# Attention and feed-forward layer in one kernel: softmax shifts transposed in groups of two pairs of heads, shorter leads, beginning reordered

## The reference

```python
x = query                                        # (32, 256, 128) float32
h = (x - mean(x)) / sqrt(var(x) + 1e-5)
q = einsum('bnd,hde->bhne', h, Wq) / 8           # 16 heads of 64
k = einsum('bmd,hde->bhme', h, Wk)
v = einsum('bmd,hde->bhme', h, Wv)
attn = softmax(einsum('bhne,bhme->bhnm', q, k), axis=-1)
o = einsum('bhnm,bhme->bnhe', attn, v)
x = x + dot(swapaxes(o, -1, -2).reshape(B, N, 1024), Wp) + bp
y = layernorm(layernorm_plain(x)) * ln1_g + ln1_b
y = gelu_tanh(y @ ternary(w1).T + b1)            # hidden width 512
y = layernorm(y) * ln2_g + ln2_b
x = x + y @ ternary(w2).T + b2                   # ternary(w): -1, 0 or 1 times mean |w|
```

## Time and profile before

| | us |
|---|---|
| median of 3 runs | 1002.18 (1001.26 to 1003.38) |
| span of the profiled execution, first to last instruction | 998.7 |
| PE busy | 980.8 (98%) |
| DVE busy | 880.0 (88%) |
| POOL busy | 837.1 (84%) |
| ACT busy | 729.6 (73%) |

### The profile page before, as it was taken

How to read it: one execution, slowest core, us unless ns; L and a number is a source line. 1 busy time by engine, 2 the same in 40 slices (tenths; PEclk the granted TensorE clock), 3 DMA queues, 4 the chain that set the end, 5 groups by cost and what they waited for, 6 DMA issues and landing times.

```text
span 998.7 us, 39391 instructions
## 1 busy us (share of the span) xinstructions
PE 980.8 (98%) x16052; PEld 782.2 (78%) x16052; DVE 880.0 (88%) x1779; ACT 729.6 (73%) x1151; POOL 837.1 (84%) x861
## 2 busy tenths in 40 slices
PE   7899999999999999999999999999999999999998
PEld 6577777778777787887887777888878777788886
DVE  7888988988889888898889988889889988788998
ACT  5687677777767777777777777777777776879995
POOL 6789888989887888888899888888888889866765
PEclk9999999999999999999999999999999999999999
DMA  6112332222331232233222233324222233354343
GB/s 141 38 32 51 53 66 45 43 49 52 74 53 27 51 73 53 52 53 71 55 48 41 48 73 51 53 53 71 46 41 47 52 52 53 69 86 75 77 86 65
DMA packets 203682, 57.82 MB, mean 58 GB/s; under 512 B 185072, under 2 KB 203248, under 8 KB 203504
## 3 DMA queue, kind: packets, MB, share of 16 engines
q1 hardware_dynamic: 201424, 54.79, 29.8%
q10 hardware_dynamic: 2080, 0.52, 0.2%
HBM read 7.21 MB, written 4.19 MB: 11 GB/s over the span
## 4 chain that ended last, share of the span: by engine, by line
PE 95%; DVE 2%; ACT 1%; issue 1%; POOL 1%; DVEq 0%; POOLq 0%; ACTq 0%
PE S L675 11%; PE PV L700 8%; PE M L635 7%; PE PV L702 6%; PE PV L701 6%; PE QK L622 5%; PE QK L623 5%; PE QK L624 5%; PE misc L675 5%; PE S L667 5%; PE S L864 3%; PE M L753 2%; PE M L718 2%; PE M L754 2%; PE M L755 2%; PE misc L667 2%
## 5 line engine op out<-in xcount | busy, mean ns | idle before, releaser
L1210 POOL TENSOR_TENSOR pl<-p 128x1024 f16<-128x1024 f32 x253 | 476.9, 1896 | 39.3 <-ACT p L1000 39.1
L1410 DVE TENSOR_REDUCE negmax<-M 128x4 f32<-128x1024 f32 x252 | 306.8, 1217 | 22.4 <-PE M L635 16.4
L1008 ACT ACTIVATE QKh<-QK 128x512 f16<-128x512 f32 x251 | 149.5, 596 | 155.5 <-PE QK L624 155.3
L1000 ACT ACTIVATE p<-S,s_exp 128x1024 f32<-128x1024 f32 x173 | 192.4, 1112 | 71.8 <-PE S L675 71.2
L700 PEld LDWEIGHTS PV<-V,p 128*128 128x128 bf16 x2048 | 186.8, 98 | 46.4 <-issue 34.5
L700 PE MATMUL PV<-V,p 128*128 128x65 f16 x2048 | 214.9, 194 | 4.0 <-DVE O L1424 2.9
L701 PE MATMUL PV<-V,p 128*128 128x64 f16 x2048 | 213.4, 193 | 0.0
L702 PE MATMUL PV<-V,pl 128*128 128x65 f16 x2048 | 212.6, 194 | 0.0
L1430 DVE TENSOR_TENSOR QKl<-QK,QKh 128x512 f16<-128x512 f32 x251 | 172.4, 687 | 42.2 <-ACT QKh L1008 41.1
L701 PEld LDWEIGHTS PV<-V,p 128*128 128x128 bf16 x2048 | 189.1, 97 | 4.7
L702 PEld LDWEIGHTS PV<-V,pl 128*128 128x128 f16 x2048 | 188.7, 97 | 0.0
(11 more groups left out here) (236 smaller groups left out, 2501.6 us busy)
## 6 DMA issues: line engine op xcount, KB each, us to landing
result<-X SPq DMA_DIRECT2D x15, 256.0 KB, 2.6
X<-in_L_attn_query SPq DMA_DIRECT2D x7, 512.0 KB, 4.8
OT<-O SPq DMA_TRANSPOSE x64, 4.6
shift<-negmax SPq DMA_TRANSPOSE x63, 2.3
O<-in_L_attn_Wk ACTq DMA_DIRECT2D x2, 256.0 KB, 4.3
O<-in_L_attn_Wq SPq DMA_DIRECT2D x2, 256.0 KB, 4.5
O<-in_L_attn_Wv SPq DMA_DIRECT2D x1, 512.0 KB, 3.9
w<-in_L_ffn_w SPq DMA_DIRECT2D x2, 256.0 KB, 5.6
```

The source lines that it names most:

```text
L1000: e.activation(p32[r][:, :, :, :].rearrange("p i m n -> p (i m n)"), score_bank(p)[:, :], ACT.Exp, scale=s_exp[:, :]).then_inc(s_ex, 1)
L1210: e.tensor_tensor(pl[r][:, :, :, :].rearrange("p i m n -> p (i m n)"), p32[r][:, :, :, :].rearrange("p i m n -> p (i m n)"), p_high(r).rea ...
L1410: e.tensor_reduce(dst[:, :, NB * jj:NB * jj + NB], max_bank(p)[:, :].rearrange("p (i t m) -> p i t m", i=2, t=NB), AX.X, ALU.max, negate=T ...
```

## The change

Groups have two pairs in place of four (`GP`). Queries and keys are computed five pairs ahead in place of seven, maxima four in place of six. Before step 0 three further pairs are started (`FIRST`) in place of five. The constants that hang on these move with them: `PAIRED`, `LOW_ON_DVE`, the banks of the first pairs. In the beginning ACT scales and splits the weight pieces 2 and 3 earlier and rounds pairs in another order; the statistics and the split of batch 2's input move from steps 0 to 5 to steps 4 to 7; the reduction of the projection weights (`part_p`, `part_g`) moves from the beginning into step 9, and turning and spreading follow in steps 10 and 11 in place of 7 and 8. `shift_in` becomes a semaphore for each buffer.

```diff
-GP = 4
+GP = 2
-Q_LEAD, MAX_LEAD, PV_LAG = 7, 6, 3
+Q_LEAD, MAX_LEAD, PV_LAG = 5, 4, 3
-PAIRED = NP - 6
+PAIRED = NP - 4
-LOW_ON_DVE = (NP - 5, NP - 3, NP - 1)
+LOW_ON_DVE = (NP - 3, NP - 1)
-MAXIMA = {"pg": (None, 7, 8), "t1": (45, 46, 54)}
+MAXIMA = {"pg": (9, 10, 11), "t1": (45, 46, 54)}
-FIRST = 5
+FIRST = 3
@@ def qk_pairs(t):
-    first = {0: [5, 6], 1: [7, 8], 2: [9], TWO_1: []}
+    first = {0: [4, 5], TWO_1: []}
@@ def max_pairs(t):
-    first = {0: ([], [5]), 1: ([6], [7])}
+    first = {0: ([], [3]), 1: ([4], [5])}
@@ def x_stats_batch(b, j):
-    return b + 2 if j == (2 if in_two(HP * b) else 0) and 1 <= b + 2 < B else None
+    return b + 2 if j == (2 if in_two(HP * b) else 0 if b else 4) and 1 <= b + 2 < B else None
...
@@ def qk_bank(p):
-            return PV if p in (1, 4, 6, 8) else QK
+            return PV if p in (1, 4) else QK
@@ def scores(p):
-                    e.wait_ge(shift_in, 16 * g)
+                    e.wait_ge(shift_in[g % 2], shift_turned(g))
@@ pe_program, beginning
+            max_scores(2)
             queries_keys(3)
-            max_scores(2)
-            e.wait_ge(s_mx, 2)
-            kept_busy(3)
-            max_scores(3)
-            queries_keys(4)
             first_shift_turned()
-            max_scores(4)
@@ act_program, beginning
             qk_high(0)
+            w_high(2)
             qk_high(1)
             qk_high(2)
-            w_high(2)
+            w_high(3)
+            first_shift()
             qk_high(3)
             x_high(1)
-            qk_high(4)
-            w_high(3)
-            first_shift()
@@ pool_program, beginning
             w_low(2)
+            w_low(3)
             x_low(1)
-            w_low(3)
-            add_bp(0)
...
+            add_bp(0)
             add_bp(1)
@@ dve_program, beginning
             max_out(2)
-            max_out(3)
-            max_out(4)
-            for p in range(2, FIRST):
-                qk_low(p)
-            e.wait_ge(p_in, P_IN)
-            largest_of(3, t2_rows(Wp), "part_p")
-            e.wait_ge(ffn_in, FFN_IN)
-            largest_of(4, g2[:, :], "part_g")
+            qk_low(2)
+            qk_low(3)
```

More of the change, by code:

```diff
@@ L104, in x_stats_batch @@
 def x_stats_batch(b, j):
-    return b + 2 if j == (2 if in_two(HP * b) else 0) and 1 <= b + 2 < B else None
+    return b + 2 if j == (2 if in_two(HP * b) else 0 if b else 4) and 1 <= b + 2 < B else None
 def x_norm_tile(b, j):
-    return (b + 2, j - 1) if j in (1, 2) and 2 <= b + 2 < B else None
+    first = 1 if b else 5
+    return (b + 2, j - first) if j in (first, first + 1) and 2 <= b + 2 < B else None
 def x_split_batch(b, j):
-    return b + 2 if j == (5 if in_two(HP * b) else 3) and 1 <= b + 2 < B else None
+    return b + 2 if j == (5 if in_two(HP * b) else 3 if b else 7) and 1 <= b + 2 < B else None
 def x_bias_batch(b, j):
-    return b + 2 if j == (7 if in_two(HP * b) else 5) and 1 <= b + 2 < B else None
+    return b + 2 if j == (7 if in_two(HP * b) or b == 0 else 5) and 1 <= b + 2 < B else None
 def two_values(t):
@@ L244, in qk_bank_before @@
 def qk_bank_before(p):
-    first = {0: None, 1: None, 2: None, 3: 0, 4: 1, 5: 3, 6: 4, 7: 5, 8: 6, 9: 7, 10: 9}
+    first = {0: None, 1: None, 2: None, 3: 0, 4: 1, 5: 3, 6: 5}
     return first.get(p, p - 1)
@@ L347, in layer @@
         ot_in = [sem(f"s_outputs_transposed{c}") for c in range(H // HH)]
-        xt_in, shift_in = sem("s_x_transposed"), sem("s_shift_transposed")
+        xt_in = sem("s_x_transposed")
+        shift_in = [sem(f"s_shift_transposed{i}") for i in range(2)]
         yt_in = [sem(f"s_ffn_y_transposed{i}") for i in range(2)]
@@ L409, in qk_bank @@
                 return misc_banks[misc_bank_no("qk", 2)]
-            return PV if p in (1, 4, 6, 8) else QK
+            return PV if p in (1, 4) else QK
         def max_bank(p):
-            return S if p in (1, 3) else M
+            return S if p == 1 else M
         def score_bank(p):
@@ L429, in two_free, with shift_turned @@
             return (s_x0, first_tiles(b)) if tile == 0 else (s_x1, b + 1)
+        def shift_turned(g):
+            return 16 * ((g + 1) // 2)
         def head_rows(i):
@@ L531, in turn_shift @@
                 e.dma_start_transpose(shift[g % 2][:, :].unsqueeze(1),
-                                      negmax16[g % 2][:, :, :].rearrange("p i c -> p (i c)")).then_inc(shift_in, 16)
+                                      negmax16[g % 2][:, :, :].rearrange("p i c -> p (i c)")).then_inc(shift_in[g % 2], 16)
             def turn_y(g):
@@ L692, in weighted @@
                 else:
-                    e.wait_ge(s_qklo, 9)
+                    e.wait_ge(s_qklo, 5)
                 for t in range(NB):
@@ L986, in shift_rounded @@
                 if g >= 3:
-                    e.wait_ge(shift_in, 16 * (g - 2))
+                    e.wait_ge(shift_in[g % 2], shift_turned(g - 2))
                 elif g == 1:
@@ L1472, in weights @@
             def weights(t):
+                if t == MAXIMA["pg"][0]:
+                    e.wait_ge(p_in, P_IN)
+                    largest_of(3, t2_rows(Wp), "part_p")
+                    e.wait_ge(ffn_in, FFN_IN)
+                    largest_of(4, g2[:, :], "part_g")
                 if t == SUMS:
```

## The result

Over 20 executions each the changed kernel took 1003.27 us (1001.69 to 1005.81) against 1001.42 (1000.80 to 1003.38): a ratio of 1.0018 with an interval of 1.0012 to 1.0024. The forecast was 1000.1, faster. The change is slower by 1.9 us, where it should have won 2.1.

The account below looks back on a forecast made before the run. PE was taken as the bound, busy 99.79 of 100 us in the middle. Terms -1.9 + 0 + 0.1 - 0.3 = -2.1 took the span from 998.7 to 996.6, time 1000.1 us; range 998.0 to 1003.0.

Parts of the forecast that it names:

- The middle and the added groups: Full steps: 64 more groups' roundings and shift transposes cost 0, since PE stays full and shifts land in time.
- Rival B: Double steps: added shift transposes land late behind transposes of outputs, making scores wait; 1006 us, chance 0.10.
- The end: Last steps: two steps with neither maxima nor queries and keys go, saving 0.3 us.
- The 1.15: PE's wait at 876.89 for DVE's division behind the last pair's low part, expected to stay.
- rival D: Other waits go too, the 1.15 in the end and some for the division; 998.6 us, chance 0.13.
- The beginning: Ramp up to pair 4's scores: earlier first shift and less work ahead, net gain 1.9 us, bounds 0.5 and 3.
- All times below include it: Start: the half-sized fill of `sel` brings the path 0.2 us forward, bounds 0 and 0.6, included in later ramp times.
- the chain: Hand-written ramp order over DVE, ACT and PE: scores of pair 0 at 18.9, first exponential 23.05, pair 4 at 34.6.
- Scores of pair 4 at 36: Sign in the ramp that only 0.5 of the 1.9 us gain stays, against 34.6 if the forecast was right.
- rival C: Beginning hangs on DVE and the rounding before the first exponential, so 0.5 of 1.9 stays; 1001.5 us, chance 0.17.
- Steps 4 to 14: Moved reductions eat DVE's slack, 0.3 us lost; ACT's later scaling of `Wp` gives 0.2 back; net loss 0.1.
- The base: Distance of 3.5 us between the profiled span and the median time, kept to turn span 996.6 into 1000.1.

Follow-up runs that it names:

- aligned: Changed kernel with 64 unused bytes per partition ahead of O, which then begins at a multiple of 256 bytes again; 1000.61 us, 0.9991 of before.
- before_off: Kernel before with 192 unused bytes per partition ahead of O, moving it off a multiple of 256 bytes; 1002.25 us, 1.0012 of before.
- three: Changed kernel with O aligned, group 1's shift transfer ahead of the feed-forward loads, and 22 unused matmuls before pair 1's scores; 999.89 us, 0.9985 of before.
- pg_first: Kernel three with the maxima of projection weights and gains taken from step 9 to steps 0 and 2; 999.82 us, 0.9982 of before.
- pg_back: Kernel pg_first with turning and spreading of the projection weights' maximum put back from steps 10 and 11 to 7 and 8; 998.76 us, 0.9977 of before.
- filler: Changed kernel with 22 unused matmuls on PE in the idle gap ahead of pair 1's scores; 1001.93 us, 1.0008 of before.
- shift_first: Changed kernel with group 1's shift transpose issued on SP ahead of the six feed-forward loads instead of behind them; 1002.02 us, 1.0007 of before.

## Why the prediction was wrong, step by step

The forecast span was 996.6 and the profiled one is 999.8, 3.2 us longer. The terms below account for it: 2.1 in the beginning, 1.0 in the steps up to pair 24, 0.1 in the middle.

- **The middle and the added groups (0):** right. +0.10 over 223 pairs, the shift landed in 2.3, at most 4.1, and no `scores` waited for it there. Behind a transpose of outputs issued at 404.51 and landed 3.8 later, the shift issued at 406.27 landed 2.3 later too, as without one ahead. Rival B is out.
- **The end (-0.3):** right, -0.30. The 1.15 stayed as 1.14, so the wait of rival D did not go.
- **The beginning (-1.9):** the step that failed; measured, it is +0.2 (1.19 - 1.01). It is wrong by two terms that were not in its sum. First, the start of pair 0: "All times below include it" puts it 0.2 before the old one, at 11.84, and the bounds of 0 and 0.6 know only the fill of `sel`. It started at 13.23, 1.4 later, because shrinking `sel` and `negmax` also moved O off its boundary (aligned, before_off). No row of before could show this, but the sizes in the code could. The 0.2 itself was right: in aligned and three that start is 11.78 and 11.83. Second, the chain left out SP: the transpose behind the six loads cost 0.56 of waiting for pair 2. Everything else in the chain held: pair 0's scores were 1.36 late (20.26 for 18.9), the first exponential 1.45 (24.50 for 23.05), pair 1's scores 1.54, pair 2's 2.13 and pair 4's 2.05 (36.65 for 34.6), and in three, with both causes mended, pair 4's came at 34.71. Scores of pair 4 at 36 were named as the sign of rival C, a chain that slips on DVE and ACT; the sign came, but not for that reason.
- **Steps 4 to 14 (+0.1 net loss):** mis-sized, +1.12 up to pair 24. The edit priced was DVE's 1.4 us of reductions; moving these away gave back 0.1 to 0.3 (pg_first). The cost was in what hangs on them. "ACT scales `Wp` in step 12 instead of 9; I take 0.2 back" had the wrong sign: steps 8 and 10 did give back 0.3 (7 and 11 took it again), but steps 13 and 14 took 0.56 more, and POOL's low part of `Wp`, which cost 0.56 in step 19, was not in the sum at all. Undoing that placement gave 0.7 (pg_back against pg_first).
- **The granted clock, which no term held:** the chain itself had a gap of 2.7 us on PE and I priced it only as time. Over its executions after's median span is 2.2 longer than before's (1001.0 for 998.8), of which 0.9 is there at full clock too; the other 1.3 is lost clock.
- **The base:** 3.5 us were added between span and time, from three executions. The executions at full clock have about 2.2. The rest is most likely lost clock of before's three executions, whose clocks are not on record. By luck this surplus of 1.3 is about what after lost through its clock: 999.8 + 3.5 is 1003.3, the measured median. So the forecast's miss is that of its span.

Which share of after's lost clock belongs to the wait for the weights and which to the gap is not settled apart. With the gap filled and the wait left (filler) the mean span lies 0.5 above the full span, with the wait mended and the gap left (aligned) 0.4, with both left 1.4, and with neither (three) 0.1. In before_off, which has the wait and not the gap, it is 0.7, and in before, which has neither, 0.6; where before loses it is not known.

## What to carry to other kernels

When a change makes a tile smaller, work out where every tile behind it now begins: here 256-byte pieces lost a quarter of their rate 192 bytes behind a multiple of 256. Price a gap on TensorE at the start also by what it does to the granted clock, and read that from many executions, since one profile may be of the lucky ones. When a step of weight preparation is moved, follow all that hangs on it, to the last engine. On the queue that issues DMAs, look at what stands ahead of the urgent one.

## What the runs showed of the hardware

- Writing 256-byte pieces 192 bytes behind a multiple of 256 in SBUF ran at 217 GB/s in place of 285 to 290 with 16 DMA engines. This holds in both kernels: after against aligned, and before_off against before.
- The granted clock fell behind a stretch in which PE was little busy (shift_first, 1.32 of 4 us: 0.68 in the next window), but it does not in every execution: after's profile has 1.72 of 4 us in that stretch and 1.00 behind it. Spans of after lie between 999.5 and 1003.5, those of three, which keeps its clock, between 997.6 and 997.9.
